# The experts' lower product in 16-bit halves, split by GpSimd: a fused sequence block on one core

## The reference

```
hid = gelu(einsum('bsd,edf->bsef', h, w1) + b1)      # 8 experts, 128 -> 512
exp_out = einsum('bsef,efd->bsed', hid, w2) + b2     # 512 -> 128: the lower product
moe = einsum('bse,bsed->bsd', gate, exp_out)
```

## Time and profile before

| | us |
|---|---|
| median of 3 runs (lowest, highest) | 1163.9 (1157.93, 1164.41) |
| span of the profiled execution, first to last instruction | 1155.9 |
| TensorE matmuls busy | 1097.5 (95%) |
| VectorE busy | 980.3 (85%) |
| ScalarE busy | 786.9 (68%) |
| GpSimd busy | 269.4 (23%) |

### The profile page before, as it was taken

The page is one execution under the profiler, slowest core; times in us unless marked ns, Lnnn a source line. Parts: engine busy times, 40 slices in busy tenths (PEclk is TensorE's granted clock), DMA queues, the critical chain, the costliest instruction groups (busy, mean ns, idle before and its releaser), DMA issues.

```text
span 1155.9 us, 27543 instructions
## 1 busy us (share of the span) xinstructions
PE 1097.5 (95%) x10435; PEld 915.9 (79%) x10435; DVE 980.3 (85%) x2576; ACT 786.9 (68%) x1772; POOL 269.4 (23%) x324
## 2 busy tenths in 40 slices
PE   4885999999999999999999999999999999999997
PEld 1573788888878888887888888788887888888897
DVE  7779789898898989889898988989899898988663
ACT  5582857768486775948667595866758587685553
POOL 2040312314041231404123130412303132130200
PEclk9795999999999999999999999999999999999899
DMA  7001000000000000000000000000000000000000
GB/s 204 6 1 41 6 6 11 1 11 6 6 11 2 15 2 11 6 6 11 1 16 2 6 10 7 11 1 15 2 6 10 6 11 1 11 2 1 11 2 10
DMA packets 18722, 14.60 MB, mean 13 GB/s; under 512 B 2408, under 2 KB 16160, under 8 KB 18592
## 3 DMA queue, kind: packets, MB, share of 16 engines
q1 hardware_dynamic: 17680, 12.76, 3.7%
q10 hardware_dynamic: 912, 0.09, 0.1%
HBM read 10.75 MB, written 2.10 MB: 11 GB/s over the span
## 4 chain that ended last, share of the span: by engine, by line
PE 86%; DVE 6%; issue 3%; POOL 2%; ACT 1%; POOLq 0%; DVEq 0%; ACTq 0%
PE O L539 19%; PE O L444 15%; PE S L427 7%; PE S L460 5%; PE U L523 5%; PE U L521 5%; PE U L522 5%; PE J L369 5%; PE J L332 4%; PE S L391 3%; PE J L333 3%; PE J L334 3%; PE S L387 3%; PE O L451 3%; DVE mxn L1048 1%
## 5 line engine op out<-in xcount | busy, mean ns | idle before, releaser
L743 ACT ACTIVATE hid<-U,b1c 128x256 f32<-128x256 f32 x512 | 200.6, 474 | 176.9 <-PE U L523 176.7
L539 PE MATMUL O<-w2s,hid 128*128 128x128 f32 x2048 | 251.0, 276 | 0.0
L539 PEld LDWEIGHTS O<-w2s,hid 128*128 128x128 f32 x2048 | 238.6, 192 | 2.9
L444 PEld LDWEIGHTS O<-Vx,P 128*128 128x128 f32 x1536 | 188.6, 192 | 35.3 <-issue 11.0
L444 PE MATMUL O<-Vx,P 128*128 128x66 f32 x1536 | 188.8, 273 | 11.5 <-ACT OT L722 9.0
L1150 DVE TENSOR_TENSOR_SCAN st<-aexp,u 128x256 f32<-128x256 f32 x256 | 175.5, 686 | 2.1 <-ACT aexp L728 2.0
L869 POOL TENSOR_TENSOR raw<-raw,nr 128x512 f32<-128x512 f32 x120 | 122.0, 1042 | 135.8 <-DVE nr L1013 135.8
L716 ACT ACTIVATE P<-S 128x768 f32<-128x768 f32 x128 | 103.7, 810 | 52.8 <-PE S L427 51.1
L877 POOL TENSOR_SCALAR_AFFINE_SELECT P<-P 128x512 f32<-128x512 f32 x128 | 90.9, 710 | 191.9 <-ACT P L716 191.9
L523 PE MATMUL U<-h2h,w1l 128*128 128x256 f16 x480 | 131.4, 274 | 0.0
L522 PE MATMUL U<-h2l,w1h 128*128 128x256 f16 x480 | 131.4, 274 | 0.0
(11 more groups left out here) (193 smaller groups left out, 2116.2 us busy)
## 6 DMA issues: line engine op xcount, KB each, us to landing
xin<-in_L_attn_x SPq DMA_DIRECT2D x16, 128.0 KB, 2.2
xres<-in_L_attn_x SPq DMA_DIRECT2D x16, 128.0 KB, 2.1
hid<-in_L_ffn_w SPq DMA_DIRECT2D x2, 1024.0 KB, 6.5
out_dram<-fin SPq DMA_DIRECT2D x16, 128.0 KB, 1.8
raw<-in_L_ffn_Wq SPq DMA_DIRECT2D x1, 512.0 KB, 4.4
raw<-in_L_ffn_Wk SPq DMA_DIRECT2D x1, 512.0 KB, 5.6
raw<-in_L_ffn_Wv SPq DMA_DIRECT2D x1, 512.0 KB, 6.5
wos<-in_L_ffn_Wo SPq DMA_DIRECT2D x1, 512.0 KB, 11.0
```

The costliest lines, as they stand in the source:

```text
L444: last = mm(dst, P32[:, p % 3, a, c0:c0 + P], Vx[:, kb, 2 * p + a, :], start=(kb == 0), stop=(kb == t))
L539: last = mm(O[e % 2][:, t * P:(t + 1) * P], hid[:, e % 2, m, t * P:(t + 1) * P], w2s[:, e * FC + m, :], start=(m == 0), stop=(m == FC - 1))
L743: fn(hid[:, e % 2, f % FC, :], U[q % 2][:, m * SEQ:(m + 1) * SEQ], ACT.Gelu_apprx_tanh, bias=b1c[:, f:f + 1], scale=1.0 / WS).then_inc(gel ...
```

## The change

The lower product is computed like the upper one: `hid` and `w2` are each kept as a high and a low 16-bit half, and a 32-bit matmul becomes three 16-bit ones (high by high, high by low, low by high). w2 is split once, in the prologue, by three GpSimd instructions of 4096 elements for each partition, in `aexp` as scratch; it is scaled by 64 there, and the gates by 1/64. The halves of `hid` are made by GpSimd in the m steps, for each half expert a copy to 16 bits (`hidden_high`) and a subtraction (`hidden_low`), both 128x512; for the last sequence VectorE makes the high half. TensorE's upper product of expert m+1 now stands in step m, where that of expert m stood, and ScalarE takes the gelus before the high halves of q and k.

```diff
-        w2s = sb("w2s", [P, NE * FC, D])
+        w2h = sb("w2h", [P, NE * FC, D], F16)
+        w2l = sb("w2l", [P, NE * FC, D], F16)
+        hidh = sb("hidh", [P, 2, FC, SEQ], F16)
+        hidl = sb("hidl", [P, 2, FC, SEQ], F16)
...
             def expert_down(s, e, weighed):
-                pe.wait_ge(gelu_done, s * NE * FC + FC * (e + 1))
+                pe.wait_ge(hid_low, s * NE * 2 + 2 * (e + 1))
...
-                        last = mm(O[e % 2][:, t * P:(t + 1) * P], hid[:, e % 2, m, t * P:(t + 1) * P],
-                                  w2s[:, e * FC + m, :], start=(m == 0), stop=(m == FC - 1))
+                        mm(dst, hi, w2h[:, e * FC + m, :], start=(m == 0), stop=False)
+                        mm(dst, hi, w2l[:, e * FC + m, :], start=False, stop=False)
+                        last = mm(dst, lo, w2h[:, e * FC + m, :], start=False, stop=(m == FC - 1))
...
-                pe.wait_ge(d_w2, 16)
+                pe.wait_ge(w2_split, 3)
...
-                    if old and 1 <= m < NE:
-                        expert_up(i - 1, m)
+                    if old and m + 1 < NE:
+                        expert_up(i - 1, m + 1)
...
             def gelus(s, e):
-                    if q % 2 == 0 and e >= 2:
-                        act.wait_ge(w2_ready, s * NE + e - 1)
+                    from_one(act, hid_low, s * NE * 2 + q - 3)
...
+            def split_w2():
+                pool.wait_ge(d_w2, 16)
+                nc.gpsimd.tensor_scalar(W232, W232, WS, None, ALU.mult).then_inc(w2_split, 1)
+                pool.wait_ge(w2_split, 1)
+                nc.gpsimd.tensor_copy(w2h[:, :, :].rearrange("p c n -> p (c n)"), W232).then_inc(w2_split, 1)
+                pool.wait_ge(w2_split, 2)
+                nc.gpsimd.tensor_tensor(w2l[:, :, :].rearrange("p c n -> p (c n)"), W232,
+                                        w2h[:, :, :].rearrange("p c n -> p (c n)"), ALU.subtract
+                                        ).then_inc(w2_split, 1)
+
+            def hidden_high(s, q):
+                e, r = divmod(q, 2)
+                pool.wait_ge(gelu_done, s * NE * FC + 2 * (q + 1))
+                from_one(pool, w2_ready, s * NE + e - 1)
+                nc.gpsimd.tensor_copy(hidh[:, e % 2, 2 * r:2 * r + 2, :], hid[:, e % 2, 2 * r:2 * r + 2, :]
+                                      ).then_inc(hid_high, 1)
+
+            def hidden_low(s, q):
+                e, r = divmod(q, 2)
+                pool.wait_ge(hid_high, s * NE * 2 + q + 1)
+                nc.gpsimd.tensor_tensor(hidl[:, e % 2, 2 * r:2 * r + 2, :], hid[:, e % 2, 2 * r:2 * r + 2, :],
+                                        hidh[:, e % 2, 2 * r:2 * r + 2, :], ALU.subtract).then_inc(hid_low, 1)
...
-                if new:
-                    for n in range(4):
-                        units(i + 1, 1, n)
+                for e in range(NE):
+                    if old:
+                        for q in (2 * e, 2 * e + 1):
+                            hidden_high(i - 1, q)
+                            hidden_low(i - 1, q)
+                    if new and e < 2:
+                        units(i + 1, 1, 2 * e)
+                        units(i + 1, 1, 2 * e + 1)
...
             def tail():
                 x_bias(LAST)
-                root_o(LAST)
-                root_e(LAST - 1)
+                for q in range(2 * NE):
+                    hidden_low(LAST, q)
+                    if q == 1:
+                        root_e(LAST - 1)
                 root_e(LAST)
```

More of the change, by code:

```diff
@@ L167, in build @@
         W132 = hid[:, :, :, :].rearrange("p r c n -> p (r c n)")
+        W232 = aexp[:, :, :].rearrange("p d n -> p (d n)")
         sel32 = P32[:, :, :, :].rearrange("p r a n -> p (r a n)")[:, 0:8 * P].rearrange("p (h k) -> p h k", h=8)
@@ L184, in build @@
             wo_ready wo_copied o_vec o_root o_act o_tr o_gate o_gT o_b2
-            w1_ready gelu_done w2_ready acc_done
+            w1_ready gelu_done hid_high hid_low w2_ready acc_done w2_split
             c_vec dt_ready tanh_done a_done scan_done y_done
@@ L195, in build @@
          wo_ready, wo_copied, o_vec, o_root, o_act, o_tr, o_gate, o_gT, o_b2,
-         w1_ready, gelu_done, w2_ready, acc_done,
+         w1_ready, gelu_done, hid_high, hid_low, w2_ready, acc_done, w2_split,
          c_vec, dt_ready, tanh_done, a_done, scan_done, y_done,
@@ L290, in prologue @@
                 sp.dma_start(gbrow[:, :], gate_b.partition_broadcast(P)).then_inc(d_small, 16)
-                sp.dma_start(w2s[:, :, :].rearrange("p (e c) n -> p e c n", e=NE),
+                sp.dma_start(W232.rearrange("p (e c n) -> p e c n", e=NE, c=FC),
                              w2.rearrange("e (c p) n -> p e c n", p=P)).then_inc(d_w2, 16)
@@ L538, in expert_down @@
                     for m in range(FC):
-                        last = mm(O[e % 2][:, t * P:(t + 1) * P], hid[:, e % 2, m, t * P:(t + 1) * P],
-                                  w2s[:, e * FC + m, :], start=(m == 0), stop=(m == FC - 1))
+                        dst = O[e % 2][:, t * P:(t + 1) * P]
+                        hi, lo = hidh[:, e % 2, m, t * P:(t + 1) * P], hidl[:, e % 2, m, t * P:(t + 1) * P]
+                        mm(dst, hi, w2h[:, e * FC + m, :], start=(m == 0), stop=False)
+                        mm(dst, hi, w2l[:, e * FC + m, :], start=False, stop=False)
+                        last = mm(dst, lo, w2h[:, e * FC + m, :], start=False, stop=(m == FC - 1))
                 last.then_inc(w2_ready, 1)
@@ L727, in decay @@
                     act.wait_ge(c_vec, s * KC + 5)
+                if s == 0 and d == 0:
+                    act.wait_ge(w2_split, 3)
                 fn(aexp[:, d, :], dt[:, :], ACT.Exp, scale=negA[:, d:d + 1]).then_inc(a_done, 1)
@@ L829, in body @@
                         with_gelu_and_tanh()
+                    if old and 1 <= m < NE:
+                        gelus(i - 1, m)
                     if new and m > 0 and m in TURN_AT:
@@ L832, in body @@
                         high(i + 1, TURN_AT[m] + 1)
-                    if old and 1 <= m < NE:
-                        gelus(i - 1, m)
                     if new and m == 8:
@@ L911, in prologue @@
                 root_g(1)
+                split_w2()
             def body(i, older, old, new, newer):
@@ L927, in body @@
                         units(i + 1, 0, 2 * k - 11)
-                if new:
-                    for n in range(4):
-                        units(i + 1, 1, n)
+                for e in range(NE):
[6 more added lines that the diff above has]
+                        units(i + 1, 1, 2 * e + 1)
+                    if not new and e == 1:
+                        root_o(i)
             def tail():
                 x_bias(LAST)
-                root_o(LAST)
-                root_e(LAST - 1)
+                for q in range(2 * NE):
+                    hidden_low(LAST, q)
+                    if q == 1:
+                        root_e(LAST - 1)
                 root_e(LAST)
@@ L1103, in o_step @@
                     for t in range(T):
-                        V.tensor_scalar(gates_of(s)[:, t, 0:NE], ge[:, t, :], grs[:, t:t + 1], None, ALU.mult
-                                        ).then_inc(o_vec, 1)
+                        V.tensor_scalar(gates_of(s)[:, t, 0:NE], ge[:, t, :], grs[:, t:t + 1], 1.0 / WS,
+                                        ALU.mult, ALU.mult).then_inc(o_vec, 1)
                 elif n == 14:
@@ L1123, in add_expert, with hidden_high @@
                                            ).then_inc(acc_done, 1)
+            def hidden_high(s, q):
+                e, r = divmod(q, 2)
+                dve.wait_ge(gelu_done, s * NE * FC + 2 * (q + 1))
+                dve.wait_ge(w2_ready, s * NE + e - 1)
+                V.tensor_copy(hidh[:, e % 2, 2 * r:2 * r + 2, :], hid[:, e % 2, 2 * r:2 * r + 2, :]
+                              ).then_inc(hid_high, 1)
             def convolve(s, n):
@@ L1221, in prologue @@
                 V.tensor_tensor(bc[:, :], bs[:, :], cs[:, :], ALU.mult)
+                V.tensor_scalar(b2s[:, :], b2s[:, :], WS, None, ALU.mult)
                 for j in range(NJ):
@@ L1362, in tail @@
                 E_TAIL = {0: (0, 1, 2), 1: (5, 6), 2: (7,)}
+                hidden_high(LAST, 0)
+                hidden_high(LAST, 1)
                 for e in range(NE):
+                    if e + 1 < NE:
+                        hidden_high(LAST, 2 * e + 2)
+                        hidden_high(LAST, 2 * e + 3)
                     for n in E_TAIL.get(e, ()):
```

## The result

The changed kernel takes 1292.3 us (median of 4 runs, 1291.0 to 1292.6). The kernel before, in runs of the same chip, takes 1164.2 (1157.9 to 1164.7). The ratio is 1.113, 95% interval 1.110 to 1.117: slower, by about 128 us. The forecast was 1335, with a range of 1230 to 1410.

A forecast was written before the change was run, and what follows sets the result against it. TensorE was taken to bound the kernel (busy 95%), with VectorE having only 4.3 us to spare in the m steps. Bodies 154, last body 7, prologue 13 and tail 2 add 176 to 1158: 1335 us stated, range 1230 to 1410.

The forecast's parts named there:

- The main case: m steps and prologue: GpSimd's new work binds and shuts VectorE out of SBUF; 1335 us, chance 0.68.
- TensorE's lower product: m steps: 24 16-bit pairs 0.058 us apart take 1.39 us instead of 1.79, 0.40 less an expert.
- rival 2: m steps: GpSimd's pairs stay ahead of TensorE, so 51 comes off and 13 goes on; 1120 us, chance 0.07.
- GpSimd's prices: m steps: cast 0.63, subtraction 1.15, semaphore 0.14, so a pair 1.92 us and sixteen 30.7.
- The holds: m steps: VectorE and GpSimd exclude each other from SBUF; GpSimd needs 42.6 us, VectorE loses 11.8 a body.
- The chain of a body: Full bodies: GpSimd's and VectorE's chains come out near each other, 11 us longer a body, 154 for fourteen.
- the first chain: m steps: GpSimd finishes its halves late, TensorE waits about 1.5 us each step; a body 10.6 us longer.
- The last body: Last body without units: 7 us longer; the tail's last cast and subtractions add 2.
- The upper product a step forward: m steps: same work, gelus reach GpSimd one step earlier, covered because GpSimd is behind; costs nothing.
- Prologue: GpSimd's three w2 instructions shut VectorE's raw out of SBUF; 13 us, bounds 0 and 17.
- Rival 4: m steps: TensorE's new gaps drop its clock to 1.2 GHz, 5 us more a body; 1410 us, chance 0.09.
- The signs: GpSimd over 700 us, subtraction waits about 1.5, scans and add_states 0.5 longer, period about 79, lower product 1.39.

The follow-up runs named there:

- experiment 7: Changed kernel with w2 split off GpSimd, gelus written in 16 bits, low half left out, no GpSimd halves, old upper-product and gelu order: 1113.9 us, 0.962.
- experiment 11: experiment 3 with the old order of upper product and gelus, GpSimd's pairs still running unread: 1256.5 us, 1.084.
- experiment 1: Changed kernel with w2 in its own buffer, high half made by ScalarE in the prologue, low half by VectorE in the first body: 1273.9 us, 1.097.
- experiment 3: experiment 2 plus GpSimd's 16 pairs of cast and subtraction a body, written where nobody reads: 1260.0 us, 1.084.
- experiment 6: Changed kernel with the old order: expert m's upper product at m step m, gelus behind the high halves: 1299.6 us, 1.122.
- experiment 5: Kernel before with the change's order alone: upper product a step forward, gelus ahead of the high halves, 32-bit lower product: 1211.0 us, 1.044.
- experiment 2: experiment 1 with gelus written directly in 16 bits, no GpSimd halves, third product reading the high half again: 1164.4 us, 1.003.
- experiment 10: experiment 5 with three buffers for hid instead of two: 1183.2 us, 1.018.

## Why the prediction was right, and where its sizes were off

The main case was right in its mechanism: GpSimd's new work holds VectorE up and is late itself. It came out 43 us too high, in one term: the fourteen bodies are 98.9 us longer and not 154. The other terms were too small, the prologue by 7.4 us and what follows the last start by 5.4, and so hid 13 us of that miss.

- **TensorE's lower product.** 1.39 us was forecast, it is 1.36 (24 pairs, from 647.62 to 648.98). The nearest row was the right guide. The 81 ns of the Trainium skill's page "TensorE: Matmul & The Clock Gate", section "Back-to-back issue gap", does not hold for this stream, in which two of every three pairs bring new weights. And experiment 7 shows that the gain is real, 44 us of the 51 that rival 2 had.
- **GpSimd's prices.** Cast 0.61 (forecast 0.63) and subtraction 1.15 (1.15) are on the mark. A pair is 1.78, not 1.92: the next cast starts 1.10 after the subtraction's start, and the semaphore between the two costs 0.08, not 0.14.
- **The holds.** Here the sizes failed. GpSimd ran from 619.6 to 655.9, 36.4 us where 42.6 were forecast. 16 by 1.78 and the `units` are 32.5, so VectorE held it for 3.9 and not 7.8. In the other direction VectorE loses 7.5 us a body (105.7 us of busy time over the fourteen full bodies, with the same 2193 instructions; 19.3 more are the prologue's and 19.0 come after the last output projection, with the 10.5 of the casts), where 11.8 were forecast. In the m steps of one body a scan loses 0.35 (0.45 forecast), and an `add_state` 0.30 (0.65 forecast). The step that failed is the `add_state`'s, in both directions. Four of the m steps show why (scans at 632.93, 642.71, 648.64 and 653.11). The scan holds the cast back by 0.40. The `add_state` then comes in near the end of that cast, loses 0.17, and holds the next subtraction back by 0.06 or 0.07, not 0.35:

```profile
642.71 1.29 DVE L1201 TENSOR_TENSOR_SCAN st<-aexp,u 128x256 f32<-128x256 f32 x1
644.03 0.65 DVE L1211 SCALAR_TENSOR_TENSOR y<-st,bc,y 128x256 f32<-128x256 f32 x1
...
643.39 1.01 POOL L905 CAST hidh<-hid 128x512 f16<-128x512 f32 x1
644.48 1.22 POOL L911 TENSOR_TENSOR hidl<-hid,hidh 128x512 f16<-128x512 f32 x1
```

- **The chain of a body.** 6.8 us, not 11: the term of 154 measured 98.9. The two chains were said to be near each other. From m step 5 on it is VectorE's that binds: GpSimd is done at 655.9, TensorE waits 2.09 us for maxima at 651.68, and the last matmul of the m steps starts at 659.13. Experiment 11 confirms it from the other side: the 7 us more of VectorE are there when nobody waits for `hidl`. And experiments 1 and 3 show that in these bodies the lateness, the first chain, costs next to nothing. The VectorE chain's own sum was 11.8 of losses less 4.3 of room plus a start up to 2 later. It measured 7.3 of losses less 0.7 of room: two errors that partly cancel, so that the forecast was nearer than its parts.
- **The last body:** the m steps of it and the tail are 14.4 us longer, against 7 and 2. In runs the last sequence costs more than that, since the quicker product gave some back: 7 us for the order (experiments 11 and 3) and 11 for its split (3 and 1).
- **The upper product a step forward costs nothing.** Right for this kernel (experiment 6: it gains 7), and for the reason given, that GpSimd is behind. What the prediction did not see is that the price is 53 us as soon as GpSimd's splitting no longer frees `hid` (experiment 5). That is a wait that another part of the same change took away.
- **Prologue.** 13 forecast, bounds 0 and 17; it is 20.4. The hold was right. The term that failed is the scaling of w2 by 64: 10.55 us for 4096 elements in place of 3.8. The cast (3.60) and the subtraction (8.25) were in their bounds. VectorE's `nu` stood until 32.42, not quite the 34.10 at which the scaling ended. `raw` ran from 33.59 to 47.25, one piece of it for 8.41, as long as the subtraction. The rule of the Trainium skill's "SBUF — State Buffer", section "SBUF: two separate sides", that the lock is held for the whole instruction, agrees with these sizes to 2 us: by it, with the three instructions ending at 46.10 instead of `raw` starting at 25.09, the term would be an estimated 21. The scaling fits least: two instructions with two inputs each ran at their usual 0.19 us within its last 1.7 us.
- **Rival 4, the clock.** It fell to 0.50 near the end of the m steps in twelve of the fourteen full bodies, for 3.4 to 6.8 us, and for 17 in the last of them (0.97 over the 43.3 us above). A clock below 1.00 in the m steps was named as a sign of being wrong, and it is there; but the rival's price is not. The two bodies at full clock (the first row is one) are as long as the next one at 0.98, and the three with 6.8 us take 74.9 to 75.0:

```profile
766.00:840.70 74.70, 64.91 (x719) 53.08 (x718) 68.01 (x160) 48.58 (x111) 48.21 (x52) 1.00 0.02 7
915.40:990.00 74.60, 66.40 (x718) 54.54 (x717) 67.61 (x160) 48.50 (x111) 48.29 (x52) 0.98 0.02 7
```

- The signs: GpSimd 776 (over 700), lower product 1.36; but scans and `add_state`s of the m steps gained 0.35 and 0.30, not 0.5, the period is 74.8, not 79, and TensorE waits for the maxima more than for the subtraction.

## What to carry to other kernels

Before giving GpSimd work because it is idle, count what VectorE reads from SBUF in that stretch, and what VectorE has to spare there. Up to the spare time the holds were nearly free (casts alone: 33 us of holds, 9 us of time), beyond it they came in full, and with them the wait for whatever stood behind the new work in GpSimd's own queue. Read an instruction's growth in the stretch where the change works: over the whole span the `add_state`s grew by 0.17 us, in the m steps by 0.30. When one part of a change measures as worth nothing, look into its waits before believing it: experiment 2 hid 50 us behind a double buffer that the rest of the change had relieved.

## What the runs showed of the hardware

- Beside GpSimd's casts and subtractions only instructions of VectorE that read SBUF alone got longer: in the m steps of one body scans from 682 to 1027 ns, `add_state`s from 485 to 782, `z` from 344 to 973. Those that read PSUM kept their length, also where they read SBUF as well: maxima 551 and 547 ns, `KTl` 681 and 679, the gated sum of the experts 347 and 341.
- A cast of 128x512 to 16 bits took 0.61 us on GpSimd and 0.42 on VectorE, the subtraction 1.15 and 0.68. At 4096 elements the in-place scaling took 10.55 us on GpSimd, 2.9 times the cast and 1.3 times the subtraction that reads two inputs.
- 16-bit pairs of weight load and 128 columns ran 56 ns apart, 24 in a row, with changing weights.
- In the profiled executions of experiments 5 and 10 TensorE's clock was at 1.2 GHz for 37.5 us in one stretch of the last body, just after a wait of 1.13 us. The kernel before has the same wait and 20 us at full clock after it, then 6.8 us at 1.2 GHz.
- In the changed kernel stretches of 3.4 us at 1.2 GHz near the end of the m steps cost no time that shows: bodies with and without them take 74.6 to 75.0 us.
